# Both ends of a one-core state-space kernel put back in their plain order, with every group's u x D left to TensorE

## What is computed

```python
def step(h, inp):
    d, b, c, ut = inp
    dA = jnp.exp(d[:, :, None] * A)                    # decay
    h = dA * h + (d * ut)[:, :, None] * b[:, None, :]  # state, 256 x 16
    y = jnp.einsum('bdn,bn->bd', h, c)
    return (h, y)
...
return ys.transpose(1, 0, 2) + u * D                   # the skip term u x D
```

## Time and profile before

| | |
|---|---|
| median of 3 runs | 1061.58 us (1057.41 to 1061.61) |
| the profiled execution | 1059.2 us |
| its span, first to last instruction | 1057.0 us |
| first scan of group 0 starts | 31.06 us |
| first scan of group 1 / of group 8 | 107.67 / 923.33 us |
| last scan unit's product ends (VectorE) | 1000.64 us |
| VectorE busy | 920.4 us (87%) |
| TensorE / GpSimd / ScalarE busy | 944.2 / 855.6 / 779.4 us |

### The profile page before, as it was taken

How to read it: one execution, slowest core, us unless ns; L and a number is a source line. 1 busy time by engine, 2 the same in 40 slices (tenths; PEclk the granted TensorE clock), 3 DMA queues, 4 the chain that set the end, 5 groups by cost and what they waited for, 6 DMA issues and landing times.

```text
span 1057.0 us, 13719 instructions
## 1 busy us (share of the span) xinstructions
PE 944.2 (89%) x4320; PEld 603.2 (57%) x4320; DVE 920.4 (87%) x722; ACT 779.4 (74%) x1241; POOL 855.6 (81%) x428
## 2 busy tenths in 40 slices
PE   4698688879989999999999999989889987998897
PEld 3455456656645566555755575546655575556556
DVE  1988999999999999999999999898999999978701
ACT  4858767878598868987788869886687867777522
POOL 0777999989987998989897999899788898866400
PEclk9797699889999999999999999999999998999999
DMA  3855655673556645755456464664646564555100
GB/s 114 285 177 198 203 164 165 178 210 103 181 166 189 190 130 150 239 146 169 164 178 202 117 190 154 194 178 130 158 134 184 159 187 130 142 172 150 39 1 16
DMA packets 97670, 167.43 MB, mean 158 GB/s; under 512 B 9920, under 2 KB 33408, under 8 KB 97344
## 3 DMA queue, kind: packets, MB, share of 16 engines
q1 hardware_dynamic: 97600, 166.57, 52.6%
HBM read 159.19 MB, written 7.34 MB: 158 GB/s over the span
## 4 chain that ended last, share of the span: by engine, by line
PE 44%; ACT 17%; issue 16%; DVE 14%; POOL 8%; DMA 1%; SPq 0%; DVEq 0%; POOLq 0%; ACTq 0%
DVE bank_d L980 9%; PE bank_y L1274 9%; PE bank_m L1104 8%; PE bank_m L1180 7%; POOL state L595 5%; PE bank_m L1187 5%; ACT bank_d L745 4%; ACT L626 4%; PE bank_m L1153 3%; DVE state L978 2%; POOL state L600 2%; PE bank_m L1194 2%; PE bank_m L1162 2%; PE bank_m L1169 2%; PE bank_m L1122 1%
## 5 line engine op out<-in xcount | busy, mean ns | idle before, releaser
L595 POOL TENSOR_TENSOR state<-du,b_rows 128x1024 f32<-128x1024 f32 (+1 forms) x288 | 629.1, 2210 | 53.6 <-PE bank_y L1274 46.1
L980 DVE TENSOR_TENSOR_SCAN bank_d<-bank_d,state 128x1024 f32<-128x1024 f32 (+1 forms) x225 | 461.2, 2050 | 32.0 <-ACT bank_d L745 30.9
L745 ACT ACTIVATE bank_d<-delta,a_neg 128x512 f32<-128x512 f32 (+1 forms) x540 | 322.6, 634 | 78.2 <-DVE state L985 73.5
L1274 PEld LDWEIGHTS bank_y<-ident,state 128*128 128x128 f32 x2048 | 243.9, 147 | 92.5 <-issue 63.4
L1274 PE MATMUL bank_y<-ident,state 128*128 128x128 f32 x2048 | 270.2, 284 | 25.9 <-DVE gated L996 12.5
L985 DVE TENSOR_TENSOR state<-bank_d,c_rows 128x1024 f32<-128x1024 f32 (+1 forms) x225 | 248.8, 1106 | 7.7
L600 POOL TENSOR_TENSOR state<-state,c_rows 128x1024 f32<-128x1024 f32 (+1 forms) x63 | 134.1, 2128 | 16.7 <-DVE state L978 15.7
L1104 PE MATMUL bank_m<-xnT,w_conv 128*128 128x508 f32 (+7 forms) x288 | 118.4, 557 | 4.5 <-DVE x1T L1005 2.4
L1187 PE MATMUL bank_m<-hidA,h_s 128*128 128x512 f32 (+1 forms) x256 | 112.5, 585 | 5.7 <-ACT hidA L817 4.6
L1180 PE MATMUL bank_m<-hidB,h_s 128*128 128x512 f32 (+1 forms) x256 | 107.8, 573 | 0.8 <-DVE hidB L1019 0.8
L978 DVE TENSOR_TENSOR_SCAN state<-bank_d,state 128x1024 f32<-128x1024 f32 (+1 forms) x45 | 92.0, 2044 | 3.4 <-ACT bank_d L745 3.4
(11 more groups left out here) (152 smaller groups left out, 1047.6 us busy)
## 6 DMA issues: line engine op xcount, KB each, us to landing
b_rows<-bc_store SPq DMA_DIRECT2D x256, 256.0 KB, 5.0
c_rows<-bc_store SPq DMA_DIRECT2D x256, 256.0 KB, 4.7
wsel<-merged SPq DMA_DIRECT2D x32, 512.0 KB, 3.5
merged<-hidA SPq DMA_DIRECT2D x8, 512.0 KB, 3.1
h_s<-in_h SPq DMA_DIRECT2D x2, 1024.0 KB, 9.2
xin<-in_x SPq DMA_DIRECT2D x7, 256.0 KB, 5.1
out<-cT SPq DMA_DIRECT2D x7, 256.0 KB, 5.3
wsel<-in_factors SPq DMA_DIRECT2D x8, 160.0 KB, 3.5
```

Of the source, the lines that this page charges most:

```text
L595: nc.gpsimd.tensor_tensor(split(unit_state(u)), du[:, d, :, :width(g)], per_half(b_rows, u), ALU.mult).then_inc(S.bx_ready, 1)
L745: ins = act.activation(split(unit_decay(u))[:, h], delta[:, d, h, :width(g)], ACT.Exp, scale=a_neg[:, h, n:n + 1])
L980: dve.tensor_tensor_scan(decay, decay, drive, 0.0, ALU.mult, ALU.add).then_inc(S.scanned, 1)
L1274: ins = pe.matmul(bank_y[:, h, s * P:(s + 1) * P], split(unit_state(u))[:, h, s * LEN:(s + 1) * LEN], ident[:, :], start=(n == 0 and s == ...
```

## The change

What it does:

- The tables hold other slots (nearly all within one unit of the old ones in the middle groups), `SECOND_GROUP` is gone, and keys with a direction (`softplus:0`) no longer have an effect. `POOL_UNITS` moves from 3 and 26 to 2 and 24.
- Group 0 fills z and the reverse projections among the forward ones, all ahead of `dbc0`; `first_inputs` is gone, so GpSimd makes `delta` and `du`; `conv_weights` and `skip_weights` run ahead of the first rotation. Silu of the reverse u is in its take.
- u x D is TensorE's in all nine groups; the sigmoid of the last group uses exp and ln as the others do.
- `h2` of group 7 is taken plain and has a gelu of its own, and stands on TensorE ahead of the whole back end of group 8.

```diff
-POOL_UNITS = (3, 8, 12, 17, 21, 26, 30)
+POOL_UNITS = (2, 8, 12, 17, 21, 24, 30)
...
-BY_SCALAR = NG - 2
-DIRECT = {"gate": NG - 1, "h1_": NG - 1, "h2_": NG - 2}
+DIRECT = {"gate": NG - 1, "h1_": NG - 1, "h2_": NG - 1}
...
-    shifts = {0: FIRST_GROUP, 1: SECOND_GROUP, NG - 2: NEXT_TO_LAST, NG - 1: LAST_GROUP}.get(g, {})
-    return at + shifts.get(name, 0.0) + (0.0 if k is None else shifts.get(f"{name}:{k}", 0.0))
+    shifts = {0: FIRST_GROUP, NG - 2: NEXT_TO_LAST, NG - 1: LAST_GROUP}.get(g, {})
+    return at + shifts.get(name, 0.0)
...
             def step_sizes(g, d):
-                if g + d == 0:
-                    return
...
-            def first_inputs():
-
-                w = width(0)
-                dve.wait_ge(S.log_ready, 1)
-                dve.tensor_tensor(delta[:, 0, :, :w], relu_dt[:, :, :w], log_dt[:, :, :w], ALU.add).then_inc(S.delta_ready, 1)
-                dve.wait_ge(S.delta_ready, 1)
-                wait_u(dve, 0, 0)
-                dve.tensor_tensor(du[:, 0, :, :w], delta[:, 0, :, :w], u_f[:, 0, :, :w], ALU.mult).then_inc(S.du_ready, 1)
...
             rotation_tables()
+            conv_weights()
+            skip_weights()
...
-                if g == NG - 1:
-                    return act.activation(t, bank(g, "glu1"), ACT.Tanh, scale=0.5, bias=hb[:, 0:1])
-                return act.activation(t, bank(g, "glu1"), ACT.Exp, scale=-1.0, bias=hb[:, 1:2])
+                return act.activation(rooms(g)[2][:, :width(g)], bank(g, "glu1"), ACT.Exp, scale=-1.0, bias=hb[:, 1:2])
...
-                if n == NST - 1 and g >= BY_SCALAR:
-                    pe.wait_ge(S.skipped, 2 * (g - BY_SCALAR) + d + 1)
...
-                    if g < BY_SCALAR:
-                        pe.matmul(bank_y[:, h, :w], skip[:, h], (u_f, u_r)[d][:, g % 2, h, :w], start=True, stop=False, skip_group_check=True)
+                    pe.matmul(bank_y[:, h, :w], skip[:, h], (u_f, u_r)[d][:, g % 2, h, :w], start=True, stop=False, skip_group_check=True)
```

More of the change, by code:

```diff
@@ L60 @@
+AHEAD = (8, 17)
+AHEAD_LEAD = 5
+FILL = {"norm": -27.0, "uf0": -23.0, "uf1": -21.0, "ur0": -24.0, "ur1": -17.5, "z0": -19.5, "z1": -20.5, "dbc0": -9.0,
[4 rows of a table added]
+SETUP = {"fuse": -4.5, "wi0": 1.0, "wo0": 1.5, "wi1": -10.5, "wo1": 6.5, "wi2": 13.0, "wo2": 12.5, "wi3": 10.0,
+         "wo3": 13.0, "wi4": 17.0, "wo4": 20.5, "wi5": 20.5, "wo5": 21.5, "wi6": 24.0, "wo6": 24.5, "wi7": 26.5,
          "wo7": 25.5}
 MERGE_LAG = 2
-TAKE_LAG = {"uf0": 1.5, "uf1": 1.5, "ur0": 1.0, "ur1": 2.5, "dbc0": 0.5, "dbc1": 0.5, "h1_0": 0.5, "h1_1": 0.5,
-            "h1_2": 1.5, "h1_3": 2.0, "h2_0": 0.5, "h2_1": 0.0, "h2_2": -4.0, "h2_3": 0.5, "out": 1.0, "wo": 2.5}
@@ L66 @@
-ACT_AT = {"scale": -36.5, "normalise": -27.5, "softplus": (-6.0, 4.0), "copied": (18.5, 32.5), "front": -10.5,
-          "silu": 52.0, "skip": (12.5, 24.5), "sigmoid": 42.0, "gelu": (61.5, 70.5)}
+TAKE_LAG = {"uf0": 1.5, "uf1": 1.5, "ur0": -11.0, "ur1": 3.0, "dbc0": 0.0, "dbc1": 0.5, "h1_0": 0.5, "h1_1": 0.5,
+            "h1_2": 1.5, "h1_3": 2.0, "h2_0": 0.5, "h2_1": 0.5, "h2_2": -2.0, "h2_3": 1.0, "out": 1.0, "wo": 2.5}
+ACT_AT = {"scale": -36.5, "normalise": -29.0, "softplus": (-6.0, 3.5), "copied": (18.5, 33.0), "silu": (-10.5, 52.0),
+          "sigmoid": 42.0, "gelu": (62.0, 70.0)}
@@ L68 @@
 DECAY_LEAD = 2
-VEC = {"rotate": -31.5, "gated": (20.5, 36.0), "x1": 44.5, "up0": 53.0, "up1": 53.5, "up2": 54.5, "up3": 54.5,
-       "w3": 74.0}
-GPS = {"power": -32.5, "residual": -11.5, "delta": (-4.0, 5.0), "inputs": (-3.5, 8.0)}
+VEC = {"rotate": -32.0, "gated": (20.5, 36.5), "x1": 44.5, "up0": 53.0, "up1": 53.5, "up2": 54.0, "up3": 54.0,
+       "w3": 74.5}
+GPS = {"power": -32.5, "residual": -12.5, "delta": (-4.0, 5.5), "inputs": (-3.5, 7.5)}
 BX_LEAD, WEIGH_LAG = 3, 1
 SUM_LAG, HELD = 2, 3
-TURN = (19.0, 36.0)
@@ L96 @@
-LAST_GROUP = {"up0": 2.5, "uf1": 5.5, "h2_2": 9.5, "delta": -1, "ur0": 1.0, "h2_0": 18.0, "h2_1": 21.0, "h2_3": 10.0,
[4 rows of a table removed]
-              "scale": 0.5, "glu1": -1.0, "store": 5.5, "norm": 0, "back": 2.5, "selected:2": 5.0, "gated:1": -1.5,
[4 rows of a table removed]
-SECOND_GROUP = {"scale": 4.0, "rotate": 2.5, "power": 3.0, "residual": -3.0, "back": 3, "store": 4, "z0": 4.5, "hid3": 2,
[7 rows of a table removed]
-NEXT_TO_LAST = {"res": 0.0, "residual": -2.5, "copied": 0.5, "h2_1": 4.5, "glu0": 0.0, "hid1": 1.5, "ur1": -1.0, "store": -5,
[7 rows of a table removed]
+FIRST_GROUP = {"ur1": -0.5, "h1_1": -1.5, "h2_0": 3.0, "power": 4.0, "bc_store": 1.0, "ur0": -2.5, "z0": -6.5, "z1": -7.0,
[5 rows of a table added]
+               "gate1": -1.5, "delta": -0.5, "inputs": -1, "normalise": -1.0, "gated": -1.5, "back": 1.5, "sigmoid": -1.5,
+               "softplus:0": 2.5, "gelu:1": 4, "silu:1": 0.5, "gelu:0": 4, "bc_store:1": 2, "copied": -1, "softplus:1": 2,
+               "inputs:1": 3.5, "copied:0": -1, "gated:1": 0.5}
@@ L210, in build @@
         halfpi_col = sb("halfpi_col", [P, 1])
-        half_col = sb("half_col", [P, 1])
         xin = sb("xin", [P, 2, 2, 2, HID])
@@ L746, in decays @@
                 ins.then_inc(S.exp_done, 1)
-            def skip(g, d):
-                wait_u(act, g, d)
-                if g > 0:
-                    wait_filled(act, g - 1, "out")
-                w = width(g)
-                for h in range(HALVES):
-                    ins = act.activation(gated[:, d, h, :w], (u_f, u_r)[d][:, g % 2, h, :w], ACT.Copy, scale=c("skip_d", h))
-                ins.then_inc(S.skipped, 1)
             def copy_y(g, d):
@@ L888, in _ @@
                 for g, rel in groups[::-1]:
-                    if rel == slot(ACT_AT, g, "front"):
+                    if rel == slot(ACT_AT, g, "silu", 0):
                         silu_front(g)
-                    if not direct(g, "gate") and rel == slot(ACT_AT, g, "silu"):
+                    if not direct(g, "gate") and rel == slot(ACT_AT, g, "silu", 1):
                         silu_gate(g)
                 for g, rel in groups[::-1]:
-                    if rel == slot(ACT_AT, g, "front"):
+                    if rel == slot(ACT_AT, g, "silu", 0):
                         silu_z(g)
@@ L1265, in sum_states @@
                     wait(pe, S.gated_ready, 2 * g + d)
-                if n == NST - 1 and g >= BY_SCALAR:
-                    pe.wait_ge(S.skipped, 2 * (g - BY_SCALAR) + d + 1)
-                    for h in range(HALVES):
-                        for s in range(sequences(g)):
-                            pe.matmul(bank_y[:, h, s * P:(s + 1) * P], gated[:, d, h, s * LEN:(s + 1) * LEN], ident[:, :],
-                                      start=False, stop=False, is_transpose=True, skip_group_check=True)
                 for h in range(HALVES):
```

57 lines of the change are left out of this document (21 added, 36 removed), and 54 rows, old and new, of tables (FILL, FIRST_GROUP, LAST_GROUP, NEXT_TO_LAST).

## The result

| | before | changed |
|---|---|---|
| time, median us | 1060.96 (4 runs, 1057.41 to 1061.61) | 1078.79 (4 runs, 1077.77 to 1083.75) |
| span of the profiled execution, us | 1057.0 | 1076.5 |
| VectorE busy, us | 920.4 | 932.5 |
| early scans of 1024 columns, 14 of them | 41.3 us | 56.4 us |

The changed kernel is slower: ratio 1.0184, 95% interval 1.0145 to 1.0223, or +17.8 us between the medians (19.5 us between the two spans). I had said +7.2 us and a range up to 1078. TensorE's mean granted clock is the same in the two profiled executions (0.953 and 0.954 of full), so it is not the clock.

A forecast was written before the change was run, and what follows sets the result against it. VectorE was taken as the bound in middle groups, with head and tail counting in full. Head 5.4, group 0 and middle groups 0 each, tail 1.8 sum to +7.2 us, giving 1068 us, range 1057 to 1078.

The forecast's parts named there:

- Middle groups: Seven middle groups: 0, from -5 to +8; GpSimd's unit moved to 24 should give back up to 1 us each.
- knots in the middle: Unit 9's copy and the h1 fill cost VectorE 1 to 1.5 us per middle group: 1077 us; chance 0.15.
- Head: Start to first scan: +5.4 us, first scan at 36.4 us, between 35 and 39.
- Term 1: Before the first scan: convolution weights ahead of the first rotation delay VectorE, +0.9 us for all that follows.
- Term 2: Before the first scan: TensorE fills two more reverse chains and two z products ahead of dbc0, +4.2 us.
- Terms 3 and 4: Before the first scan: merge wi1 behind dbc0, +0.5 us; softplus to first scan with GpSimd's delta and du, -0.2 us.
- Group 0: First scan of group 0 to that of group 1: merge waits gone, one new wait; sum 0, -3 to +2.
- The wait at unit 9: In group 0, VectorE waits for decays that stand behind the first reverse projection of group 1: 2.5 us.
- case of a half clock: In group 0, VectorE's wait at unit 9 is 4.5 us if TensorE is at half clock, 1 us at full.
- the 2.6 us of waits on them go: In group 0, VectorE's waits for expert merges vanish, as merges no longer stand right behind their fills: 2.6 us.
- Tail: From the last gelu of h1 to the end: +1.8 us, from +0.5 to +4.
- that sentence: Near the end, the sigmoid's exp, ln and table load, 2.7 us, hide behind w3; uncovered they cost 2.7 less 1.0.

The follow-up runs named there:

- experiment 1: Changed kernel, GpSimd's drive of unit 11 or 20 waiting until VectorE's early scan of unit 8 or 17 is done: 1052.3 us, ratio 0.9932 to before.
- experiment 5: Changed kernel with three TensorE fills (ur1, z0, z1) of groups 1 to 6 back at their slots of before: 1064.6 us, ratio 1.0040.
- experiment 7: Changed kernel without early decays; those of units 8 and 17 go to PSUM like all others: 1072.5 us, ratio 1.0122.
- experiment 12: Changed kernel with GpSimd's wait one product later than in experiment 1, so one drive can stand beside the early scan: 1064.7 us, ratio 1.0057.
- experiment 6: Kernel before with three TensorE fills (ur1, z0, z1) of groups 2 to 6 at the changed kernel's slots: 1062.9 us, ratio 1.0036.
- experiment 9: Kernel of experiment 1 with the convolution weights again behind the rotation of group 0's input: 1052.2 us, first scan at 34.88 instead of 34.64.
- experiment 10: Kernel of experiment 1 with group 0 by the slots of the kernel before: 1062.3 us, ratio 1.0022.
- experiment 2: Kernel before with the same GpSimd wait as experiment 1: 1053.1 us, ratio 0.9938.
- experiment 11: Kernel of experiment 1 with groups 7 and 8 by the slots of the kernel before: 1064.9 us, ratio 1.0030.
- experiment 3: Changed kernel with groups 1 to 6 by the tables of the kernel before, without group 1's own shifts: 1085.0 us, ratio 1.0231.
- experiment 4: Kernel before with groups 1 to 6 by the tables of the changed kernel: 1085.1 us, ratio 1.0216.

## Why the prediction was wrong

*Middle groups: the step that failed.* "I set **0** for seven groups, from -5 to +8." They cost 12.5 us. I took VectorE's busy time as fixed (a table that "orders the same work a little differently") and looked for change only in its waits. The waits for decays did fall, by 4.5 us, most of it at unit 27 (3.5 us before, none over 0.15 us now), as I hoped for unit 24. What grew was the duration of an instruction, by the exclusion between VectorE and GpSimd. It could have been seen beforehand: the 14 early scans of the kernel before were uneven, 2.28 to 4.49 us, where the 175 others were even, and each long one stood beside a GpSimd product. Nor did I ask which steps the words "nearly all within one unit" left out: `ur1` moved by 1.5 units and `z1` by 2. I weighed neither that row nor the order of TensorE's fills at units 11 to 15 for what it does to GpSimd. Experiments 1, 5, 7 and 12 show this cause, each by another means; that the order of three fills is enough to bring it about from the kernel before is refuted by experiment 6.

*The rival "knots in the middle"* gave 1077, near the result, but by another mechanism: waits of VectorE at unit 9 and behind h1. They did not come: unit 9 had 0.9 us of waits in seven groups before and has none now, and the waits for decays fell. Its number was right by chance.

*Head: +5.4, measured +4.0.* Term 1, the weights, was 0.9; the rotation did start at 8.01 us (7.9 said), but TensorE's first fill starts at 13.36 instead of 13.10, 0.3 us later: with the weights ahead GpSimd's power no longer loses 0.8 us beside the weight product. The weights were not hidden before, as I had it, they stood in the power's way; experiment 9 shows the first scan no earlier for having them behind. Term 2 was 4.2, and by experiment 10 the added fills are worth that. Against the kernel before, though, the way from the first fill to `dbc0` grew by 3.3 us only (7.08 to 10.35), so that `dbc0` came at 23.71 us instead of 25.3. The first 16 matmuls that I took as a base, 6.47 us, take 5.22 in the tenth experiment and 5.14 in the second, at a granted clock of 1.00 in each; what makes that difference is open. Terms 3 and 4 together were +0.3 and are +0.45: from `dbc0` to the first scan it was 10.88 us and is 11.33. (The addends of term 4 make 3.9, not 4.0.)

*Group 0: 0, measured +0.2.* The wait at unit 9 came, 1.9 us (2.5 said). Its case of a half clock did not: TensorE was granted 1.00 from 53 to 59 us, where that chain ran, as it was before; the earlier trace rows is of units 3 and 4, not of the same stage. The waits on the first merge fills did fall, from 2.6 to 0.5 us, but those on the second ones grew from 0.2 to 3.3, so "the 2.6 us of waits on them go" was wrong in sum. The other waits for decays, 4.0 us and 0.7 more at the units of GpSimd, which I had staying, fell to 2.7, and the two early scans of this group took 0.8 us less. Errors of like size met.

*Tail: +1.8, measured +3.0.* From the last gelu of h1 to the start of the last h1 fill it was 33.9 us and is 36.6 (1018.34 to 1054.93); I had 35.7. Up to `hid` the steps are right: 24.9 us from the gelu's end to its first product, 25.0 said. The excess lies behind it, 0.2 us in `hid` and `wo`, 0.7 on ScalarE and TensorE from the last take of `wo` on, and 0.3 in the last store, behind everything:

```profile
1048.42 0.38 ACT L764 ACTIVATE xnT<-bank_m 128x256 f32<-128x256 f32 x1 [2.20 <-PE bank_m L1112]
1048.82 1.28 ACT L608 ACT_TABLE_LOAD   x1
...
1050.11 0.84 ACT L767 ACTIVATE relu_dt<-bank_m,col 128x256 f32<-128x256 f32 x2
...
1054.93 7.15 PE L1130 MATMUL bank_m<-log_dt,h_s 128*128 128x256 f32 x32 [0.62 <-DVE log_dt L972]
```

The table load itself is 1.28 us with the takes right at both ends, as the row of before said. The 2.66 us that the Trainium skill ("ScalarE: Activation LUTs", section "What ACT_TABLE_LOAD costs") gives for a switch does not show here: from the end of the take before the load to the start of the take behind it, it is 1.31 us. What I gave too little is gates and ups in a row, 4.83 us from the load's end to the first h1 product, where I had 4.1. The exp and ln hid behind `w3`, as said. For the other half of that sentence, that without the cover they would cost 2.7 less 1.0, experiment 11 shows 0.9 us on the way to VectorE, not 1.7.

*Sum.* 4.0 + 0.2 + 12.5 + 2.8 against 5.4 + 0 + 0 + 1.8. Group 8 itself is neutral (78.5 us from its first scan to the gelu's end before, 78.35 now), so the 2.8 are the tail's 3.0 less 0.2. Without the collisions the rest of the change cancels out: experiments 1 and 2 are 0.8 us apart. The middle of the changed tables is then the better one: groups 1 to 7 take 804.0 us in experiment 1 and 812.2 in experiment 2, which pays for the head (4.7) and for group 8 and the tail (4.0). The kernels of the first and the ninth experiment are the fastest here, 7.2 us below the kernel before by the medians of the first's comparison.

Open: in three of seven groups (2, 4 and 7) a scan of unit 17 waited for the drive that was running and for one that started 1.8 to 2.0 us behind the scan's own start; in the others it waited for one. In group 3 (3.97 us) as in group 4 (6.30 us) the scan arrived about 0.5 us into a drive, and nothing in the rows tells them apart. The rule cited above accounts for the first product alone. The scan of unit 8 in group 6, 4.45 us in the changed kernel, stays at 4.44 in experiment 1: what it meets there is GpSimd's product `du` (2.3 us), not a drive, and a wait for that one was not tried.

## What to carry to other kernels

Before costing a change of order at nothing, look at the spread of each instruction's duration, not at its mean: an instruction that is twice as long in some groups as in others may be waiting inside itself, as here, and then its busy time moves when a neighbour moves. Where VectorE is the bound and an instruction of it has both operands in SBUF, find what GpSimd does beside it, and give GpSimd an explicit wait there rather than rely on one that happens to come from TensorE. And a hand-tuned order is a whole: four mixes of the two tuned tables (experiments 3, 4, 10 and 11) each lost 8 us or more, in their traces, in the groups at their seams.

## What was unexpected of the hardware

- A scan of 128x1024 with a decay in SBUF takes 2.28 us with GpSimd quiet, as with the decay in PSUM. Beside GpSimd's products of 2.34 us it ends 2.15 us behind the one that it waited for: 2.5 to 4.5 us with one, 6.3 to 6.5 with two. The profile counts all of it as busy.
- The exclusion goes both ways and can pay either side: GpSimd's drive took 3.80 us where it came 0.9 us behind the scan, and its two-column power took 1.54 instead of 0.71 us beside a VectorE product (that this is the same exclusion is my reading).
- A wait that looks like a loss, GpSimd's 1.9 to 2.1 us for TensorE at unit 17 of groups 3 to 5, was worth up to 4 us of VectorE's time each.
